# Macaron block on one core: routing weights of the gated feed-forwards spread through DRAM, and the loop's turning, gating and routing placed three chunks earlier

## What is computed

```
scores = softmax(xn @ gate_w.T)                     # 16 experts
keep the 2 best of 4 groups, then the 2 best experts; weight = its softmax score
h1 = xn @ We1[e] + be1[e];  h3 = xn @ We3[e] + be3[e]
y  = sum over the chosen e of weight[e] * ((silu(h1) * h3) @ We2[e] + be2[e])
y += (silu(xn @ ws1 + bs1) * (xn @ ws3 + bs3)) @ ws2 + bs2
x += 0.5 * y
```

## Time and profile before

| what | us |
|---|---|
| median of 3 runs | 3382.59 |
| lowest and highest | 3351.72, 3384.48 |
| the profiled execution's own time | 3352.73 |
| its span, first to last instruction | 3350.8 |
| mean granted TensorE clock | 0.921 of full speed |

### The profile page before, as it was taken

The page is one execution under the profiler, slowest core; times in us unless marked ns, Lnnn a source line. Parts: engine busy times, 40 slices in busy tenths (PEclk is TensorE's granted clock), DMA queues, the critical chain, the costliest instruction groups (busy, mean ns, idle before and its releaser), DMA issues. The chain is left out here.

```text
span 3350.8 us, 46737 instructions
## 1 busy us (share of the span) xinstructions
PE 2959.6 (88%) x16194; PEld 1788.4 (53%) x16194; DVE 2511.5 (75%) x6115; ACT 1760.6 (53%) x2683; POOL 904.5 (27%) x885
## 2 busy tenths in 40 slices
PE   7999969999999998899995689899799999989853
PEld 5666623443444433666664456566566666656432
DVE  6877768888888880788776797967467778787775
ACT  3444415777777775444435456455345555555544
POOL 2111022112112100211101345566323323343333
PEclk9999968999999996999995588999899999999975
DMA  2000022121222110100000000000000000000000
GB/s 76 1 1 1 1 88 86 70 93 68 81 93 78 72 49 5 51 1 1 1 1 0 1 7 19 13 20 26 32 13 13 13 7 13 13 7 26 7 7 25
DMA packets 33698, 99.03 MB, mean 30 GB/s; under 512 B 4184, under 2 KB 4792, under 8 KB 29240
## 3 DMA queue, kind: packets, MB, share of 16 engines
q1 hardware_dynamic: 31288, 91.85, 7.5%
q10 hardware_dynamic: 2176, 4.19, 0.3%
HBM read 53.56 MB, written 42.47 MB: 29 GB/s over the span
## 5 line engine op out<-in xcount | busy, mean ns | idle before, releaser
L698 DVE TENSOR_REDUCE att_mx<-att_pair 128x2 f32<-128x1024 f32 x512 | 616.8, 1219 | 124.4 <-PE att_pair L947 124.3
L873 ACT ACTIVATE att_pt<-att_pair 128x1024 f32<-128x1024 f32 x512 | 522.2, 1025 | 224.8 <-PE att_pair L957 222.7
L969 PE MATMUL att_o<-att_pt,att_vx 128*32 128x256 f32 x4096 | 327.8, 405 | 10.8 <-ACT att_oT L879 5.8
L947 PE MATMUL att_pair<-att_k,att_q 24*128 24x512 f32 x1024 | 267.5, 526 | 49.6 <-DMA att_k<-att_spread_k 14.0
L957 PE MATMUL att_pair<-att_q,att_k 26*128 26x512 f32 x1024 | 261.0, 510 | 0.0
L449 ACT ACTIVATE ffnA_h<-ffnA_up,b 128x512 f32<-128x512 f32 x144 | 99.0, 688 | 189.5 <-PE ffnA_up L105 186.0
L449 ACT ACTIVATE ffnB_h<-ffnB_up,b 128x512 f32<-128x512 f32 x144 | 99.0, 688 | 188.8 <-PE ffnB_up L105 183.6
L957 PEld LDWEIGHTS att_pair<-att_q,att_k 26*128 26x128 f32 x1024 | 96.9, 188 | 189.9 <-issue 164.1
L947 PEld LDWEIGHTS att_pair<-att_k,att_q 24*128 24x128 f32 x1024 | 98.8, 192 | 138.9 <-ACT att_pt L873 92.1
L969 PEld LDWEIGHTS att_o<-att_pt,att_vx 128*32 128x32 f32 x4096 | 90.6, 110 | 140.1 <-issue 118.6
L1889 ACT ACTIVATE att1k_sq<-att1k_k 128x512 f32<-128x512 f32 x128 | 76.2, 595 | 161.5 <-PE att1k_k L105 161.1
(11 more groups left out here) (543 smaller groups left out, 7953.4 us busy)
## 6 DMA issues: line engine op xcount, KB each, us to landing
att_q<-att_spread_q SPq DMA_DIRECT2D x16, 1024.0 KB, 5.0
att_k<-att_spread_k SPq DMA_DIRECT2D x16, 1024.0 KB, 4.8
att_spread_q<-att_qhi SPq DMA_DIRECT2D x32, 256.0 KB, 2.5
att_spread_k<-att_khi SPq DMA_DIRECT2D x32, 256.0 KB, 3.3
context<-att1k_ctx SPq DMA_DIRECT2D x16, 512.0 KB, 2.6
att1q_cin<-context SPq DMA_DIRECT2D x16, 512.0 KB, 3.3
X<-L_attn_x ACTq DMA_DIRECT2D x8, 512.0 KB, 7.6
att_spread_q<-att_qlo SPq DMA_DIRECT2D x16, 256.0 KB, 2.5
```

What stands on the lines that cost most here:

```text
L698: v.tensor_reduce(top[b % 2][:, t, h:h + 2], pair("s", k)[:, :].rearrange("p (h n) -> p h n", h=2), AX, ALU.max, negate=True).then_inc(mx, 1)
L873: a.activation(pt[k % 8][:, :, :].rearrange("p h n -> p (h n)"), pair("t", k)[:, :], ACT.Exp, scale=scale).then_inc(p_, 1)
L947: last = pe.matmul(pair("s", k)[:, (j - j0) * 512:(j - j0 + 1) * 512], qb[b % 3][r, u, t * P:(t + 1) * P], kb[b % 3][r, u, :], start=True, ...
L969: last = pe.matmul(obank[j * BLOCK:(j + 1) * BLOCK, cols], vxb[b % 3][:, t, 4 * u + j, :], pt[(2 * g + j // 2) % 8][:, j % 2, cols], start ...
```

## The change

Four things are altered in `ffn0`, and both calls have them.

1. `spread` and its bank are gone. The routing weights are now also turned in plain float32: the router writes them to columns 32 to 47 of `pairb`, the turning product has 48 rows instead of 32 and its own bank `comb`, and ScalarE copies rows 32 to 47 to `plain` in SBUF. SyncE writes `plain` (16x512) to the DRAM tensor `kept`, waits until it has landed, and reads it back in 8 transfers, each of which repeats two rows of 2 KB into 64 partitions of `weights` (four buffers of two chunks each, with the signals `cw0` to `cw3`). `weighed` multiplies by these buffers in SBUF instead of the bank `cw`.
2. Order in the loops: on TensorE `turned` goes from slot 4 to 1, `gate` from 7 to 4, `combined` from behind slot 8 to slot 6, and `back` from 2 to 5. On ScalarE `high` goes from 5 to 2, `exps` from slot 0 of the group itself to slot 5 of the group before, `combined` to slot 6, and `out` from ahead of the Silu of slot 2 to ahead of that of slot 3. On VectorE `low`, `finish`, `stats`, the start of the chain and `moments` go three slots forward, and `added` goes from 2 to 6.
3. The waits on the shared bank `misc` follow the new order.
4. Memory: the attention's weights are given back before ffnB; ffnB uses four buffers of layer 1 (`spare`) as `weights`.

```diff
--- before.py
+++ after.py
@@ -178,8 +178,7 @@
...
 ROUTING = (("e", 16), ("prob", 16), ("s", 16), ("pm", 8), ("psum", 8), ("gsum", 4), ("alt", 4), ("gs", 4), ("g1", 4),
-           ("g2", 4), ("k1", 4), ("k2", 4), ("pen", 4), ("ms", 16), ("o1", 16), ("o2", 16), ("k3", 16), ("k4", 16),
-           ("comb", 16))
+           ("g2", 4), ("k1", 4), ("k2", 4), ("pen", 4), ("ms", 16), ("o1", 16), ("o2", 16), ("k3", 16), ("k4", 16))
@@ -205,15 +204,16 @@
...
+    plain = mem.sb("plain", [3 * EXPERTS, GROUP])
+    weights = [w[:, :] for w in spare or mem.ring("weights", 4, [P, 2 * GROUP])]
+    weight = lambda c: weights[c // 2][:, c % 2 * GROUP:c % 2 * GROUP + GROUP]
+    kept = nc.dram_tensor(name + "_weights", [EXPERTS, GROUP], F32, kind="Internal").ap()
...
-    pairb = mem.ring("pairb", 2, [P, TILES, 32], F32R)
-    misc, ltb, cwb, acc = mem.ps("misc"), mem.ps("lt"), mem.ps("cw"), mem.ps("acc")
+    pairb = mem.ring("pairb", 2, [P, TILES, 3 * EXPERTS], F32R)
+    misc, ltb, combb, acc = mem.ps("misc"), mem.ps("lt"), mem.ps("comb"), mem.ps("acc")
...
-    cw_bank = lambda i, c: up[c % 4] if i == groups - 1 and c else cwb
@@ -338,16 +341,17 @@
...
-            v.wait_ge(st.sem, m)
-            m = st.at(v.tensor_tensor(r["comb"], r["o1"], r["prob"], ALU.mult))
-            yield
+            comb = pb[:, :, 32:48].bitcast(F32)
             if i >= 2:
                 v.wait_ge(S.cT, i - 1)
             v.wait_ge(st.sem, m)
-            m = st.at(v.tensor_copy(pb[:, :, 0:16], r["comb"]))
+            m = st.at(v.tensor_tensor(comb, r["o1"], r["prob"], ALU.mult))
             yield
             v.wait_ge(st.sem, m)
-            v.tensor_tensor(pb[:, :, 16:32], r["comb"], pb[:, :, 0:16].bitcast(F32), ALU.subtract).then_inc(S.comb, 1)
+            m = st.at(v.tensor_copy(pb[:, :, 0:16], comb))
+            yield
+            v.wait_ge(st.sem, m)
+            v.tensor_tensor(pb[:, :, 16:32], comb, pb[:, :, 0:16].bitcast(F32), ALU.subtract).then_inc(S.comb, 1)
@@ -361,11 +365,11 @@
...
             n, e = E9(i, c), E8(i, c)
-            v.wait_ge(S.cw, e + 1)
+            v.wait_ge(S.cw[c // 2], 32 * (i + 1))
             v.wait_ge(S.gl, n + 1)
             if e >= 4:
                 v.wait_ge(S.dn, chunk_of(e - 4) + 1)
-            v.tensor_tensor(hc[e % 4][:, :], cw_bank(i, c)[:, :], h3[n % HELD][:, :], ALU.mult).then_inc(S.hc, 1)
+            v.tensor_tensor(hc[e % 4][:, :], weight(c), h3[n % HELD][:, :], ALU.mult).then_inc(S.hc, 1)
@@ -384,18 +388,18 @@
                 if i < groups:
                     gated(i, c)
                 take(chain, 3)
-                if c == 2 and i >= 2:
+                if c == 2 and i + 1 < groups:
+                    low(i + 1)
+                if c == 3:
+                    finish(chain)
+                if c in (3, 4) and i + 2 < groups:
+                    stats(i + 2, 2 * (c - 3), 2 * (c - 3) + 2)
+                if c == 4:
+                    chain = gate(i + 1) if i + 1 < groups else iter(())
+                if c == 5 and i + 2 < groups:
+                    moments(i + 2)
+                if c == 6 and i >= 2:
                     added(i - 2)
-                if c == 5 and i + 1 < groups:
-                    low(i + 1)
-                if c == 6:
-                    finish(chain)
-                if c in (6, 7) and i + 2 < groups:
-                    stats(i + 2, 2 * (c - 6), 2 * (c - 6) + 2)
-                if c == 7:
-                    chain = gate(i + 1) if i + 1 < groups else iter(())
-                if c == 8 and i + 2 < groups:
-                    moments(i + 2)
@@ -424,9 +428,12 @@
...
         def combined(i):
             a.wait_ge(S.cT, i + 1)
+            if i:
+                a.wait_ge(S.kept, 16 * i)
+            a.activation(plain[32:48, :], combb[32:48, :], ACT.Copy).then_inc(S.plain, 1)
             if i >= 2:
                 a.wait_ge(S.dn, E9(i - 1, 0))
-            a.activation(combT[i % 2][0:32, :], misc[0:32, :], ACT.Copy).then_inc(S.ct, 1)
+            a.activation(combT[i % 2][0:32, :], combb[0:32, :], ACT.Copy).then_inc(S.ct, 1)
@@ -435,33 +442,32 @@
...
         high(0)
+        exps(0)
         for i in range(groups + 1):
             for c in range(CHUNKS):
                 n = E9(i, c)
-                if c == 2 and i >= 2:
+                if c == 3 and i >= 2:
                     out(i - 2)
-                if c == 5 and i + 1 < groups:
+                if c == 2 and i + 1 < groups:
                     high(i + 1)
                 if i < groups:
                     a.wait_ge(S.up1, n + 1)
                     if n >= 4:
                         a.wait_ge(S.gl, n - 3)
                     a.activation(h1[n % 4][:, :], up[2 * n % 4][:, :], ACT.Silu, bias=W["b13"][:, 0, c:c + 1]).then_inc(S.sil, 1)
-                if c == 0 and i < groups:
-                    exps(i)
-            if i < groups:
-                combined(i)
+                if c == 5 and i + 1 < groups:
+                    exps(i + 1)
+                if c == 6 and i < groups:
+                    combined(i)
...
     def tensor(pe):
...
         def turned(i):
             pe.wait_ge(S.xn, i + 1)
-            if i >= 3:
-                pe.wait_ge(S.add, i - 2)
-            elif i == 2:
-                pe.wait_ge(S.ct, 1)
-            elif i == 1:
-                pe.wait_ge(S.xl, 1)
+            if i >= 4:
+                pe.wait_ge(S.add, i - 3)
+            elif i:
+                pe.wait_ge(S.xl, i)
             turn(pe, misc, group(xn[i % 2][:, :]), ident).then_inc(S.xT, 1)
@@ -475,38 +481,25 @@
...
         def combined(i):
             pe.wait_ge(S.comb, i + 1)
-            if i + 1 < groups:
-                pe.wait_ge(S.xl, i + 2)
-            elif i >= 2:
-                pe.wait_ge(S.add, i - 1)
+            if i:
+                pe.wait_ge(S.ct, i)
             for t in range(TILES):
-                last = pe.transpose(misc[0:32, t * P:(t + 1) * P], pairb[i % 2][:, t, :].bitcast(F32), ident[:, :])
+                last = pe.transpose(combb[0:48, t * P:(t + 1) * P], pairb[i % 2][:, t, :].bitcast(F32), ident[:, :])
             last.then_inc(S.cT, 1)
 
         def back(i):
             pe.wait_ge(S.y, i + 1)
-            pe.wait_ge(S.ct, min(i + 2, groups))
-            if i == groups - 1 and i:
+            pe.wait_ge(S.xl, min(i + 4, groups))
+            if i:
                 pe.wait_ge(S.add, i)
             turn_back(pe, misc, yT[i % 2], ident).then_inc(S.yo, 1)
...
-        def spread(i, c):
-            e = E8(i, c)
-            if c == 0:
-                pe.wait_ge(S.ct, i + 1)
-            if i == groups - 1 and c:
...
-            pe.matmul(cw_bank(i, c)[:, :], K["spread"][:, c, :], combT[i % 2][:, :], start=True, stop=True).then_inc(S.cw, 1)
 
         def down(n):
             i, c = divmod(n, CHUNKS)
             if c == 0:
                 if i:
                     pe.wait_ge(S.y, i)
+                pe.wait_ge(S.ct, i + 1)
                 pe.matmul(acc[:, :], W["b2"][0][:, :], combT[i % 2][:, :], start=True, stop=False)
                 pe.matmul(acc[:, :], W["b2"][1][:, :], combT[i % 2][:, :], start=False, stop=False)
@@ -531,23 +524,38 @@
                     pairs3(pe, up[(2 * n + 1) % 4][:, :], [w[:, c, :] for w in W["w3"]], x).then_inc(S.up3, 1)
                 if n - 2 >= CHUNKS:
                     down(n - 2 - CHUNKS)
-                if i and c < CHUNKS - 1:
-                    spread(i - 1, c)
-                if c == 2 and i >= 2:
+                if c == 1 and i + 1 < groups:
+                    turned(i + 1)
+                if c == 4 and i + 1 < groups:
+                    gate(i + 1)
+                if c == 5 and i >= 2:
                     back(i - 2)
-                if c == 4 and i + 1 < groups:
-                    turned(i + 1)
-                if c == 7 and i + 1 < groups:
-                    gate(i + 1)
-            if i < groups:
-                combined(i)
+                if c == 6 and i < groups:
+                    combined(i)
         down(E9(groups, 0) - 2)
         down(E9(groups, 0) - 1)
         back(groups - 1)
...
+    def sync(sp):
+        if prefetch:
+            prefetch(sp)
+        halves = kept.rearrange("(c e) n -> e c n", e=2)
+        for i in range(groups):
+            sp.wait_ge(S.plain, i + 1)
+            if i:
+                for landed in S.cw:
+                    sp.wait_ge(landed, 32 * i)
+            sp.dma_start(kept, plain[32:48, :]).then_inc(S.kept, 16)
+            sp.wait_ge(S.kept, 16 * (i + 1))
+            for part, landed in enumerate(S.cw):
+                if i:
+                    sp.wait_ge(S.hc, E8(i - 1, 2 * part + 2))
+                for e in range(2):
+                    sp.dma_start(weights[part][INTER * e:INTER * (e + 1), :].rearrange("p (c n) -> p c n", c=2),
+                                 halves[e, 2 * part:2 * part + 2, :].unsqueeze(0).to_broadcast([INTER, 2, GROUP])).then_inc(landed, 16)
+
     with nc.Block() as block:
-        if prefetch:
```

(9 more changed lines are left out.)

12 lines of the change are left out of this document (4 added, 8 removed).

## The result

| what | before | after |
|---|---|---|
| median, us | 3380.8 (20 runs) | 3354.1 (20 runs) |
| lowest and highest, us | 3351.7, 3399.9 | 3324.3, 3392.6 |
| the profiled execution's own time | 3352.7 | 3353.7 |
| its mean granted TensorE clock | 0.921 | 0.908 |

What follows compares the result with a forecast made beforehand. TensorE's list, plus its waits, was taken to bound both feed-forwards. Full groups -15.1, group 15 -1.0, tail -2.0 and start +1.8 give -16.3 us a stage, -32.6 in all: 3382.6 to 3350 us, range 3300 to 3390.

Steps and rivals of the forecast that it cites:

- What bounds it: Both feed-forwards: TensorE is busy in every microsecond, so its list counts, plus what others keep it waiting.
- the spread products: TensorE's list in the loop: eight products of 0.23 us leave it, 1.87 us a group, all on the path.
- the 0.2 of waiting: TensorE's real waiting in a group, from the exponential in slot 0 delaying Silus: 0.2 us goes.
- The moved `out`: Slot 2: the bias product waits for `y`, as `out` now follows that slot's Silu: +0.91 us a group.
- The rival without this wait: Slot 2: the wait for `y` is absent or hidden, so 3325 us on the median; chance 12%.
- The full group: Loop, groups 2 to 14: from 25.60 to 24.44 us, -1.16 each, -15.1 a stage.
- The way through DRAM: Weights written and read back, 5.8 us; VectorE waits half a microsecond in slot 0; cost in the loop counted as 0.
- The slow rival: Repeated reads of the same two rows are slow; below 97 GB/s the kernel is slower, at 80 GB/s 3520 us; 12%.
- The tail: End of a stage: from 15.7 to 13.7 us, -2.0, or 0 if the parts of the weights land late.
- The start: Start of a stage: group 0's weights have no cover; between 0 and 5.8 us, taken as +1.8.
- Sum: Full groups -15.1, group 15 -1.0, tail -2.0, start +1.8: -16.3 us a stage, -32.6 for both.
- VectorE held by GpSimd: Slots 6 and 7: VectorE's operations with two SBUF inputs wait for GpSimd's normalising, giving 3385 us; chance 8%.

Runs made afterwards that it cites:

- the first two experiments: The changed kernel with `out` back ahead of the Silu of slot 2, 3329.6 us; and the change's loop order with weights still spread by products, 3373.9 us.
- the first experiment: The changed kernel with `out` put back ahead of the Silu of slot 2 and of `high`: 3329.6 us, 0.9852 to before.
- the runs of slots 7 and 8: The changed kernel with `combined` moved from slot 6 to slot 7 (3377.4 us, 1.0012 to before) or slot 8 (3469.3 us, 1.0286).
- The fourth experiment: The kernel with `out` put back, plus `combined` on TensorE in slot 5 and `plain` copied right behind the exponential: 3311.3 us, 0.981 to before.
- the run of the order alone: The changed kernel's loop order, weights still spread by products, nothing through DRAM, their turning behind slot 8: 3373.9 us, 0.9999 to before.
- the first four experiments: Against the changed kernel: `out` put back, 3329.6 us; order alone, 3373.9; weights later, 3377.4 and 3469.3; `out` back and weights earlier, 3311.3.

## Why the forecast was nearly right

- **What bounds it, the spread products, the 0.2 of waiting.** Right. Taken apart by the first two experiments the loop is 25.60, 25.32 with the order, 23.48 without the spread products.
- **The moved `out`.** Right to 0.02 us (0.91; the group 0.93), and at the instants forecast. Of what the change costs, this is the largest part: without it the change would have been worth twice as much. The rival without this wait said 3325, and the first experiment took 3330.
- **The full group.** 24.44 against 24.40: 13 groups give -15.5 instead of -15.1; group 15 -0.9.
- **The way through DRAM.** Its length was put too low: 6.6 us on the mean (6.8 in the group shown) instead of 5.8. The step that failed is the pace of the reads, for which I chose 408 GB/s between 39 and 408, from a row whose transfers write 128 partitions. It is 225. The nearest row was near in time and queue, not in shape. The loop had cover: 2.2 us spare by my count, less the missing 0.8 to 1.0 leaves 1.2 to 1.4, and the runs of slots 7 and 8 measured 1.6. So "counted at 0" held there. The slow rival's point of decision, 97 GB/s, was not reached.
- **The tail.** Forecast -2.0, measured +0.1. I counted TensorE's products and only named the late parts as a bound. At 225 GB/s a part takes 2.33 us and its two down products 1.72: it had to be read off from the same rate that I counted as hidden in the loop. The fourth experiment, with the weights earlier, has the 13.7.
- **The start.** Forecast +1.8, measured +3.35. The sum by rows: idle time 6.0 - 2.04 = +4.0; the stretch at 1.2 GHz, 3.75 us from 54.64 to 58.39 where the first experiment takes 57.38 - 55.02 = 2.36 for the same eight products, +1.4; the spread products of a group, -1.87; together +3.5. (Measured: the product at the head of group 2 ends at 70.14 before and 73.89 after, less the 0.4 by which the stage starts later.) I had no term for the router's chain of group 0, which has no earlier group to run beside and is now due three slots sooner (3.2 us idle, the same in the run of the order alone), and none for the clock. The clock's part is chance: in this execution it stayed up behind the first idle place and fell behind the second.
- **Sum.** -15.5 - 0.9 + 0.1 + 3.35 = -12.95 for ffnA, measured -12.9. ffnB, at -13.3, is alike. The two missed terms are 2.1 + 1.55 = 3.65 a stage, 7.3 for both; less the 0.6 by which the loop came out better, 6.7, and between -32.6 and -26.2 lie 6.4.
- **VectorE held by GpSimd.** It was the other way round, and at no cost. GpSimd's two operations before and after:

```profile
L154 POOL TENSOR_SCALAR ffnA_xn<-X,ffnA_mv,ffnA_rstd x52: 783/794/812, 74.9 to 384.3; 128x128 f32<-128x128 f32 x52
L148 POOL TENSOR_TENSOR ffnA_rstd<-ffnA_rstd,minus_half x13: 1028/1028/1030, 73.7 to 380.8; 128x4 f32<-128x4 f32 x13
```

```profile
L154 POOL TENSOR_SCALAR ffnA_xn<-X,ffnA_mv,ffnA_rstd x52: 788/800/1313, 69.5 to 364.7; 128x128 f32<-128x128 f32 x52
L148 POOL TENSOR_TENSOR ffnA_rstd<-ffnA_rstd,minus_half x13: 1432/1435/1457, 68.0 to 360.3; 128x4 f32<-128x4 f32 x13
```

(minimum, median, maximum in ns.) L148 takes 0.4 us longer and the longest L154 0.5, while `weighed`, now with two inputs in SBUF, keeps its 683 ns (690 before). At 213.94 L148 started inside the `weighed` that ran from 213.79 to 214.48; before, it started at 227.28 just as far inside the `weighed` that began at 227.13, which read the bank, and took 1.03. In the run of the order alone, where `weighed` reads the bank too, four L154 take 3.17 us, against 3.65. So GpSimd waits. VectorE hardly does: the router's product of line 303 of the new file, with both inputs in SBUF, started inside a running L154 in all 13 groups of the loop and took 0.19 us each time, and `weighed` took longer in one group only (0.78 us at 70.53, 0.21 behind the start of an L154 of 0.80). The Trainium skill ("SBUF — State Buffer", "SBUF: two separate sides") says that the two exclude each other for a whole instruction; the trace agrees where GpSimd is the one that waits (0.4 to 0.5 us), and does not where VectorE would have to. GpSimd has 19 us of slack a group, so it costs nothing.

## What to carry to other kernels

A saving in a loop is only the half of its ledger: walk the order of each engine for what a moved step now stands behind (one `out` behind a Silu gave back 0.93 of the loop's 2.12 us), and walk the start and the tail with the same durations, since a latency hidden in the loop is bare there. When a rate has to be borrowed from another transfer, take one with the same shape at the destination; and of a chain that is hidden, write down the spare time, since that is what tells how early its head must be moved.

## What I had not expected of the hardware

- Transfers that write 64 partitions kept the DMA engines full at 225 to 235 GB/s, transfers that write 128 at 357 GB/s, with pieces of 2 KB in both; a piece took an engine 147 ns (median) in the one and 84 in the other.
- After 2.5 us of idleness TensorE's granted clock fell to 1.2 GHz for 3.75 us in the changed kernel; after 3.2 us at 42.43 it didn't. In the first experiment it fell behind the same 3.2 us (products 0.43 apart from 42.55 to 48.26) and not behind the 1.7 us at 55.02. The same gap may thus cost some 2 us or nothing. With two slots' delay of the weights, when TensorE waited 3 to 4 us in each group, the clock fell in eight of eleven groups, and cost 1.2 to 3 us in each of them.
- The attention, untouched, ran for 897 us at a granted clock of 0.91 in the profile before and for 909 us at 0.89 after, and from 886 to 934 us in the profiles of the first four experiments. That is as much as the effect that was to be measured, and why one profile's total can't be set against another's.
